# Cross-attention's mask added to the scores by an identity product on TensorE, and the scores copied out by ScalarE

## The reference

```python
energy = jnp.einsum('bhqd,bhkd->bhqk', Q, K) * scale
energy = jnp.where(m == 0, -1e9, energy)      # m: the mask, the same for all heads
attn = jax.nn.softmax(energy, axis=-1)
out = jnp.einsum('bhqk,bhkd->bhqd', attn, V)
```

## Time and profile before

| | |
|---|---|
| median of the runs | 863.65 us |
| span of the profiled execution | 856.1 us |
| what the median has beyond that span | 7.55 us |
| TensorE busy in the span | 737.2 us (86%) |
| VectorE busy | 638.0 us (75%) |
| ScalarE busy | 488.0 us (57%) |
| GpSimd busy | 305.1 us (36%) |
| first and last scores of cross-attention | 464.7 to 608.4 us |

### The profile page before, as it was taken

How to read it: one execution, slowest core, us unless ns; L and a number is a source line. 1 busy time by engine, 2 the same in 40 slices (tenths; PEclk the granted TensorE clock), 3 DMA queues, 4 the chain that set the end, 5 groups by cost and what they waited for, 6 DMA issues and landing times.

```text
span 856.1 us, 14502 instructions
## 1 busy us (share of the span) xinstructions
PE 737.2 (86%) x4572; PEld 355.0 (41%) x4572; DVE 638.0 (75%) x1087; ACT 488.0 (57%) x982; POOL 305.1 (36%) x249
## 2 busy tenths in 40 slices
PE   6789999999999999999988889899869898789800
PEld 3442222222222222222223356566657676567600
DVE  3488888888888888777884779897927656589765
ACT  2225677777777677776776553442335666457622
POOL 8000600000000398890002465555732474444311
PEclk9898999999999999999999999897979999899965
DMA  7746040030401699883000090000141332413121
GB/s 197 185 111 159 5 94 20 19 77 17 93 20 35 147 254 276 249 258 115 2 1 1 17 375 2 0 2 1 49 148 40 92 128 89 145 48 95 58 99 49
DMA packets 51170, 80.72 MB, mean 94 GB/s; under 512 B 16469, under 2 KB 35416, under 8 KB 49690
## 3 DMA queue, kind: packets, MB, share of 16 engines
q1 hardware_dynamic: 37065, 44.91, 19.2%
q0 software_dynamic: 9952, 31.29, 11.9%
q10 hardware_dynamic: 4080, 3.61, 1.8%
HBM read 48.21 MB, written 33.11 MB: 95 GB/s over the span
## 4 chain that ended last, share of the span: by engine, by line
PE 57%; DVE 20%; DMA 6%; issue 5%; ACT 4%; POOL 4%; SPq 2%; DVEq 1%; ACTq 0%; POOLq 0%
PE bank L542 12%; PE bank L534 12%; PE quad L515 11%; PE quad L861 5%; DVE rowmax L952 5%; PE bank L878 5%; DMA kstack<-k_parts 3%; PE quad L612 2%; PE bank L466 2%; DVE hl L1182 2%; ACT probs L1488 2%; POOL x_sorted L1778 2%; DVE sc L1055 1%; DVE max L1062 1%; DMA qstack<-q_parts 1%
## 5 line engine op out<-in xcount | busy, mean ns | idle before, releaser
L952 DVE TENSOR_REDUCE rowmax<-quad 128x1 f32<-128x1024 f32 x256 | 303.1, 1219 | 75.9 <-PE quad L515 75.4
L1488 ACT ACTIVATE probs<-bank 128x512 f32<-128x512 f32 x512 | 284.2, 595 | 115.1 <-PE bank L534 112.2
L534 PE MATMUL bank<-qstack,kstack 98*128 98x512 bf16 x512 | 194.1, 387 | 11.7 <-ACT probs L1488 10.0
L515 PE MATMUL quad<-kstack,qstack 96*128 96x512 bf16 x512 | 177.7, 387 | 15.5 <-DVE rowmax L952 6.7
L861 PE MATMUL quad<-xbT,w 128*128 128x128 bf16 x1104 | 119.6, 224 | 22.5 <-DVE hl L1182 16.1
L542 PE MATMUL bank<-probs,v_all 128*32 128x512 f32 x1024 | 139.0, 611 | 0.0
L534 PEld LDWEIGHTS bank<-qstack,kstack 98*128 98x128 bf16 x512 | 49.0, 97 | 191.7 <-ACT probs L1488 162.8
L861 PEld LDWEIGHTS quad<-xbT,w 128*128 x1104 | 91.3, 100 | 53.1 <-issue 38.3
L1612 ACT ACTIVATE hid<-quad,b 128x128 f32<-128x128 f32 x184 | 52.6, 370 | 59.6 <-PE quad L861 58.0
L515 PEld LDWEIGHTS quad<-kstack,qstack 96*128 96x128 bf16 x512 | 48.5, 99 | 77.0 <-DVE rowmax L952 39.3
L1832 POOL DMA_INDIRECT y_tokens<-ysb,dest x46 | 47.3, 1029 | 82.8 <-DVE ysb L1196 75.1
(11 more groups left out here) (181 smaller groups left out, 984.6 us busy)
## 6 DMA issues: line engine op xcount, KB each, us to landing
xb<-x_sorted SPq DMA_DIRECT2D x46, 129.0 KB, 2.3
x_sorted<-blank POOLq DMA_DIRECT2D x6, 774.0 KB, 9.1
w1raw<-in_w POOLq DMA_DIRECT2D x8, 512.0 KB, 6.0
w2raw<-in_w POOLq DMA_DIRECT2D x8, 512.0 KB, 6.4
w_split<-w1two POOLq DMA_DIRECT2D x8, 512.0 KB, 5.7
w_split<-w2two POOLq DMA_DIRECT2D x8, 512.0 KB, 4.4
w<-w_split SPq DMA_DIRECT2D x16, 256.0 KB, 5.0
w<-w_split SPq DMA_DIRECT2D x4, 1024.0 KB, 11.7
```

The costliest lines, as they stand in the source:

```text
L515: mm = pe.matmul(bank[2 * (p % 2) + e], q, kstack[slot][0:MAXROW, j, e * 512:e * 512 + 512], start=True, stop=True)
L534: mm = pe.matmul(bank[4 + i % 2], kstack[slot][0:KROWS, j, kt * P:kt * P + P], qstack[slot][0:KROWS, half, j, :], start=True, stop=True)
L952: dve.tensor_reduce(rowmax[:, k % 2, p:p + 1], quad[:, 2 * (p % 2):2 * (p % 2) + 2, :].rearrange("p a n -> p (a n)"), AX_X, ALU.max).then_ ...
L1488: act.activation(probs[:, i % PR, :], bank[4 + i % 2], ACT.Exp, scale=INV4).then_inc(probs_ready, 1)
```

## The change

The mask is no longer applied by VectorE. GpSimd makes `shade`, a bfloat16 tile that is 0 where the mask is 1 and -2^100 where it is 0 (one operation instead of two, near 87 us in the self-attention). For each of the four banks of a tile TensorE first multiplies the identity with `shade`, repeated over four heads, which starts the accumulation; the scores are added to it. ScalarE copies the four banks to `sc2` (`keep_scores`), and VectorE's `take` keeps only the maximum.

```diff
@@ TensorE, scores2
                 for e in (2 * half, 2 * half + 1):
+                    pe.matmul(bank[e][:, 0:4 * SC], ident16[:, :], shade[:, n:n + 1, :].to_broadcast([P, 4, SC]), start=True, stop=False)
+                for e in (2 * half, 2 * half + 1):
                     mm = pe.matmul(bank[e][:, 0:4 * SC], q2T[:, half, i * P:i * P + P],
                                    kbd[:, g // 2, half, 4 * (e % 2):4 * (e % 2) + 4, :].rearrange("p h s -> p (h s)"),
-                                   start=True, stop=True)
+                                   start=False, stop=True)
@@ VectorE, take
-                dve.wait_ge(s2_ready, n + 1)
-                if n >= SR:
-                    dve.wait_ge(p2_turned, 3 * (n - SR) + 3)
-                dve.tensor_tensor(sc2[:, n % SR, :, :].rearrange("p (e h) s -> p e h s", e=4),
-                                  quad[:, :, 0:4 * SC].rearrange("p e (h s) -> p e h s", s=SC),
-                                  cap[:, n:n + 1, :].rearrange("p o (u s) -> p o u s", u=1).to_broadcast([P, 4, 4, SC]),
-                                  ALU.min).then_inc(s2_taken, 1)
                 if between is not None:
                     between()
                 dve.wait_ge(s2_taken, n + 1)
@@ ScalarE
+            def keep_scores(n):
+                act.wait_ge(s2_ready, n + 1)
+                if n >= SR:
+                    act.wait_ge(p2_turned, 3 * (n - SR) + 3)
+                act.activation(sc2[:, n % SR, :, :].rearrange("p (e h) s -> p e (h s)", e=4), quad[:, :, 0:4 * SC], ACT.Copy).then_inc(s2_taken, 1)
@@ ScalarE, the last unit of self-attention
+                        elif i == 4 * START2[0] + 5:
+                            keep_scores(0)
                         elif i == 4 * START2[1] + 5:
+                            keep_scores(1)
                             exp2(0)
                         elif i == 4 * START2[2] + 5:
+                            keep_scores(2)
                             exp2(1)
@@ ScalarE, the main loop, behind keep_turned(n) and keep_x1T
+                if i < 3 and n + FAR < NT:
+                    keep_scores(n + FAR)
                 if n + FAR - 1 < NT:
                     exp2(n + FAR - 1)
                 if i == 3:
                     keep_o2(g)
+                    if n + FAR < NT:
+                        keep_scores(n + FAR)
@@ GpSimd
-            step(pool.tensor_scalar(cap[:, :, :], maski[:, :, :], 0.0, -NO_CAP, ALU.is_equal, ALU.mult))
-            step(pool.tensor_scalar(cap[:, :, :], cap[:, :, :], NO_CAP, MASKED, ALU.add, ALU.add))
+            step(pool.tensor_scalar(shade[:, :, :], maski[:, :, :], 0.0, MASKED, ALU.is_equal, ALU.mult))
```

More of the change, by code:

```diff
@@ L31 @@
 INV4 = 0.25
-MASKED = -4.0e9
-NO_CAP = 3.0e38
+MASKED = -2.0 ** 100
 SR = 4
@@ L58 @@
 EC = 17
-MASK_STEPS = 9
+MASK_STEPS = 8
 SOON = 14
@@ L147, in build @@
         maski = cap[:, :, :].bitcast(I32)
+        shade = sb("shade", [P, NT, SC], BF16)
         power = sb("power", [P, NT])
```

## The result

The change makes the kernel slower: median 881.26 us (878.24 to 883.31, 4 runs) against 863.57 us for the kernel before, ratio 1.0213 [1.0183, 1.0243], or +17.7 us. Three of the four runs of the kernel before are those of the table ahead of the prediction; the fourth took 859.94 us. Measured again on two occasions it was 1.0133 [1.0078, 1.0189] and 1.0100 [1.0065, 1.0135], or +13.9 and +10.4 us between the medians. The profiled execution took 882.88 us, its span is 881.1.

The account below looks back on a forecast made before the run. The bound was taken as a loop of waits through TensorE and VectorE, neither engine alone. Terms 7.0 + 3.3 + 0.8 + 2.3 = 13.4 us took 856.1 to 869.5, plus 7.55 gave 877.0 us; range 866.5 to 884.

Parts of the forecast that it names:

- the worse one: Whole kernel: each stall with a long half-clock stretch and the masks' weight loads not hidden, +20, 884 us; chance 0.15.
- ScalarE's copy: Each of 16 copies of 1232 elements out of PSUM on ScalarE was taken as 1.23 us, 1.43 being possible.
- Masks: TensorE's 64 added matmuls: 0.13 us each, 0.52 a tile at full clock, 8.3 us in all, partly in gaps.
- Last unit: End of self-attention: copies on ScalarE delay exponentials TensorE waits for, +3.3 us, 1.3 of it half clock.
- First group: Cross-attention's first tiles: exponential 3 behind the copy of tile 4 delays sum, maximum and shift; adds 3.2 us.
- Middle group: Later group of tiles: TensorE behind from tile 10 by masks and ScalarE's copy and exponential ahead of turned probabilities; +3.3 us.
- Clock: TensorE's new stalls ahead of values2 bring half clock, about 1.2 us for each of two stalls, +2.3 us in all.
- The way out: From the last group to the experts, opened by GpSimd's scatters behind shift 14: +0.8 us.
- The step around the sum: From predicted execution to median: 7.55 us added to 869.5, as the median lies that far above the span, giving 877.0.
- Only ScalarE's block, clock kept: Rival: block costs only in the last unit and before values2, sum 3 not late; 6.6 us, 870.3 us; chance 0.20.
- Faster, VectorE was what mattered: Rival: copies slip into ScalarE's waits, TensorE's 3 us gap closes in three groups, 857 us; chance 0.10.
- No difference: Rival: masks mostly in gaps, ScalarE's block of 1 to 2 us made up by VectorE, 863 to 866 us; chance 0.10.

Follow-up runs that it names:

- masks_only: The changed kernel with VectorE instead of ScalarE copying the scores out, TensorE still adding the mask; 858.62 us against 858.49 for the kernel before, ratio 1.0016.
- gap_filled: The changed kernel plus nine unused matmuls on TensorE in its wait ahead of the last turn of tiles 3, 7 and 11; 868.19 us, 1.0130 to the kernel before.
- shift_from_psum: Masks by TensorE, no ScalarE copies; VectorE takes maximum and subtracts it straight from PSUM, GpSimd's shift dropped; ratio 0.9971 to the kernel before.
- late_fused: Masks by TensorE, no ScalarE copies; from tile 7 on VectorE takes maximum and subtracts from PSUM without GpSimd's shift; 851.85 us against 857.46 before, ratio 0.9934.

## Why the prediction was right, point by point

The forecast was 877.0 us, in 866.5 to 884.0; 881.26 came. Sign and range held; the time lies 0.3 us beyond the 873 to 881 of the likeliest case, towards the worse one. The sum of 13.4 stands against 16.7, 17.1 and 18.4 us in the stretch of the three profiles (each against the first one of before; 2.0 less against the second), and against 17.7, 13.9 and 10.4 us between the medians. The second and third profile were the slowest execution of their kernel, the first the second slowest. The mechanism was right: the waits came where they were forecast. That the sum lies in the middle of the three medians is in part luck, by the clock term and by the first measurement, whose 17.7 us may not be all kernel.

*ScalarE's copy.* 1199 ns, taken as 1230. VectorE's copy from the same banks takes 1427. The estimate stood on the exponential of the same size (1.00 ns an element); the ScalarE operation of 512 elements is not at that price, as I had it, but at 1.17 ns (600 by 512).

*Masks.* The four of a tile start in pairs, each 0.27 us before its two scores (the 322 ns of the group overlap with what follows), 0.54 us a tile at full clock against 0.52 predicted, no weight load showing.

*Last unit.* ScalarE in order of time, the change:

```profile
475.26 1.20 ACT L1489 ACTIVATE sc<-quad 128x1232 f32<-128x1232 f32 x1 [2.02 <-PE quad L614]
476.35 1.22 ACT L1496 ACTIVATE sc<-sc 128x1232 f32<-128x1232 f32 x1
477.47 2.75 ACT L1483 ACTIVATE probs<-bank 128x512 f32<-128x512 f32 x5
...
485.84 1.20 ACT L1489 ACTIVATE sc<-quad 128x1232 f32<-128x1232 f32 x1 [2.25 <-PE quad L614]
486.93 1.22 ACT L1496 ACTIVATE sc<-sc 128x1232 f32<-128x1232 f32 x1
488.05 2.75 ACT L1483 ACTIVATE probs<-bank 128x512 f32<-128x512 f32 x5
...
494.47 0.60 ACT L1576 ACTIVATE outT<-bank 128x512 f32<-128x512 f32 x1 [1.27 <-PE bank L542]
```

This is the predicted picture: a wait of 2 us for the scores, copy, exponential, then the five that TensorE waits for. With the 2.2 us that the change's profile is late at x1T, the five start 1.5 us later than 473.70 (predicted 1.7) and the next ones 4.1 later than 481.75 (predicted 4.2). outT: +4.6, +2.1, +3.4 us in the three profiles, against 3.3. At full clock on both sides it is 33.8 - 30.4 = +3.4 us, where I had 2.0: the term was 1.4 us too small there, and the 1.3 us of half clock that I had added made up for it.

*First group.* ScalarE and then VectorE in order of time:

```profile
507.69 1.20 ACT L1489 ACTIVATE sc<-quad 128x1232 f32<-128x1232 f32 x1 [1.89 <-PE quad L614]
508.78 1.22 ACT L1496 ACTIVATE sc<-sc 128x1232 f32<-128x1232 f32 x1
...
516.33 1.23 ACT L1496 ACTIVATE sc<-sc 128x1232 f32<-128x1232 f32 x1 [2.82 <-POOL sc L1794]
```

```profile
510.04 1.44 DVE L1062 TENSOR_REDUCE sum<-sc 128x16 f32<-128x1232 f32 x1 [4.80 <-ACT sc L1496]
```

Exponential 3 runs at 508.78 instead of 498.36, behind the copy of tile 4; VectorE's sum waits 4.80 us for it, and with it come late the maximum of tile 4, the shift, and exponential 4 (516.33; before 506.47). That was the chain predicted, link by link. From outT to `values2` 24.77 us against 21.46 before (509.14 less 487.68): +3.3, predicted +3.2.

*Middle group.* TensorE in order of time, the change's first and second group, and then the second group of before:

```profile
518.10 0.67 PE L632 MATMUL bank<-ident,sc 128*104 128x128 f32 x2 [2.86 <-ACT pT L1510]
519.24 7.05 PE L646 MATMUL bank<-pT,vbd 128*128 128x512 f32 x10 [0.47 <-ACT pT L1510]
...
565.14 0.62 PE L632 MATMUL bank<-ident,sc 128*104 128x128 f32 x2 [2.02 <-ACT pT L1510]
566.24 5.75 PE L646 MATMUL bank<-pT,vbd 128*128 128x512 f32 x10 [0.47 <-ACT pT L1510]
```

```profile
548.68 0.42 PE L630 MATMUL bank<-ident,sc 128*104 128x128 f32 x2 [0.25 <-ACT pT L1509]
549.58 4.56 PE L644 MATMUL bank<-pT,vbd 128*128 128x512 f32 x10 [0.47 <-ACT pT L1509]
```

`values2` starts 33.19 us after T6 (533.05), predicted 33.35 after the end of the scores ahead; TensorE goes on behind the division in the next group at 597.47, 18.75 after T10, predicted 18.85. The wait for `pT` ahead of the last turn is 2.02 us where it was 0.25 in the same group of before. What went wrong in size is the start of the comparison. I counted +2.8 from the third group's 30.55 us, but T6 to T10 holds the second group, and there `values2` starts at 549.58, which is 29.67: +3.5. With masks (0.5) and clock (1.2) that is the +5.2 of the profile.

*Clock.* This is the term that was too small, and in the wrong place. I took 1.2 us for each of two stalls. `values2` alone lost 2.5 and 1.2 us in the first profile, 2.3 and 2.8 in the third. And the part of a middle group that I put down to ScalarE's queue is for the most part clock: less what the clock lacked, T6 to T10 is 38.8 us in the change (45.67 less 0.15 of it), 37.2 before (40.44 less 0.08 of it), +1.6, of which 0.7 is masks by the 37.9 of masks_only (41.16 less 0.08 of it). The profile of gap_filled fits that from the other side: the wait is filled, not shortened, and the group takes 41.1 us; its timed median doesn't bear it out. So in the profiles a middle group of the change loses up to 2 to 5 us more by the clock (6.9 and 8.5 us lacking against 3.2 and 5.0) and about 1 by ScalarE's new waits themselves.

*The way out.* +0.5, +1.9 and +2.0 us against 0.8. Shift 14:

```profile
626.27 2.25 POOL L1794 TENSOR_TENSOR sc<-sc,max 128x1232 f32<-128x1232 f32 x1 [2.08 <-DVE max L1057]
```

18.2 us later than 608.03, 2.2 of them from ahead of the stretch; I had said some 12. That the third group costs less than the second (44.6 to 46.3 us against 41.8) and the rest is shorter by 2.3 to 2.6 us is the slack between TensorE and the scatters that I had reckoned with.

*The step around the sum.* I added 7.55 us, the median less the span, and took it for what lies around a span. That reading was wrong: 1.8 us lie around the spans of the runs here. The profile of before was an execution of about 857.9 us, and the rest is how far executions and chips differ. For that execution the sum would be 856.1 + 1.8 + 13.4 = 871.3. The sum to 877.0 is right all the same, since it is the same as 863.65 + 13.4: a difference is added to the median outright.

*The rivals.* "Only ScalarE's block, clock kept" (+6.6) is no mere rival: the change's two best executions on one chip are near it (863.5 and 864.0 us at 0.949 and 0.950, +6 us on the median of 857.46), though against the fastest execution of before, 854.88, the fastest of the change is 8.6 us longer. "Faster, VectorE was what mattered" fell with the 50.2 us that VectorE waits for the copy. "No difference" holds for the masks alone. What stays open: whether another order in ScalarE's list would bring the time back, why some executions of the same program hold the clock in the stretch and others don't, and how much of the 17.7 us of the first measurement, which had the 6 us in the experts, is the kernel and how much the clock of that occasion.

## What to carry to other kernels

Ask what stands behind a wait in the list of the engine that gets it, not how busy the engine is: ScalarE was idle more than half of the stretch and was the wrong place; in the traces its list held what TensorE wanted next. Two other orders of the list didn't mend it in the medians. Work added to TensorE in a place where it waits can be free (the masks, 0.16%): it waits anyway, and in the profile less time is at half clock. Compare several executions before you believe a profile's loss: a wait of 2 us cost more than its length in the change's profiles, and filling it gave nothing in the median. And when a pass moves or goes, look also at what ran beside it: without GpSimd's shift the two kinds of VectorE operation that had run beside it took less than half of their time.

## What the runs showed of the hardware

- A copy of 128x1232 float32 out of four PSUM banks takes ScalarE 1199 ns and VectorE 1427 ns; VectorE's maximum straight from PSUM (1427 to 1429) and its subtraction from PSUM (1441 to 1442) cost the same as from SBUF (1425 to 1436, and 1442 to 1443 for the one of tile 15).
- VectorE's operations on 128x256 beside GpSimd's shift and additions took 1193 to 1196 ns (`attn_all`) and 886 to 888 ns (`xres`, norm) each; in shift_from_psum and late_fused, without the shift, 417 to 419 and 405 to 407 ns.
- In the profile with nine bfloat16 matmuls of 462 columns (1.92 us) in a wait of some 2 us the granted clock was 1.00 behind them (558 to 562 us), and ten float32 matmuls took 4.56 us; without the nine they took 5.75 to 7.37 in the change's profiles, partly at 1.2 instead of 2.4 GHz. The timed medians of the two kernels are the same.
- Executions of one program on one chip differ in mean granted clock (0.934 to 0.950) and by 12 us with it; of the kernel before by less (0.938 to 0.948, 854.9 to 861.9 us).
- On one chip four blocks of the experts are 4.7 instead of 3.1 to 3.2 us apart, in every kernel profiled there, with a wait whose releaser the profile cannot name. The cause was not found.
